# First cross-attention's attending loop: two tiles in a row, four buffers of probabilities and values, loops unrolled

## The reference

```python
def _L0_xattn_ref(x, latents, gamma_x, beta_x, gamma_l, beta_l, Wq, Wkv, Wo):
    xn = layer_norm(x, gamma_x, beta_x)          # x: the context, 12544 x 256
    ln = layer_norm(latents, gamma_l, beta_l)    # 128 x 256
    q = (ln @ Wq).reshape(b, m, h, d)            # h = 8 heads, d = 64
    kv_x = xn @ Wkv
    k_x = rope_rotate_k(k_x)                     # the context's keys
    ...
    k = jnp.concatenate([k_x, k_l], axis=2)      # context, then latents
    v = jnp.concatenate([v_x, v_l], axis=2)
    sim = jnp.einsum('bhid,bhjd->bhij', q, k)
    attn = jax.nn.softmax(sim, axis=-1)
    out = jnp.einsum('bhij,bhjd->bhid', attn, v)
    return out @ Wo
x = x + _L0_xattn_ref(ctx_1024, _layernorm(x, axis=-1), ...)
```

## Time and profile before

| | |
|---|---|
| median of 3 executions | 2609.48 us (2606.8 to 2609.7) |
| the profiled execution | 2611.38 us, span of the trace 2609.4 us |
| the loop of `attend` in the trace | from 377.84 us (first values) to 782.97 us (end of the last sum) |
| records of values, scores and weights matmuls of context tiles | 392, 1568, 1568 |
| mean granted clock of TensorE | 0.936 of 2.4 GHz over the span |

### The profile page before, as it was taken

One profiled execution on the slowest core, in us unless ns is written; L12 is line 12 of the kernel. 1 busy time (PEld: TensorE's weight loads), 2 busy tenths in 40 slices (PEclk: granted clock), 3 DMA queues, 4 the chain that ended last, 5 costly groups with the idle time before them and its releaser, 6 DMA issues. The chain is left out here.

```text
span 2609.4 us, 57414 instructions
## 1 busy us (share of the span) xinstructions
PE 2324.1 (89%) x21898; PEld 1435.1 (55%) x21898; DVE 1837.8 (70%) x2825; ACT 1194.8 (46%) x2046; POOL 518.1 (20%) x300
## 2 busy tenths in 40 slices
PE   3999989999994969999987999999997459999979
PEld 1444446666664836666656745665555415555548
DVE  6888778988886166666634388888886777777721
ACT  4566543333334337777772333333332325556552
POOL 0555530000000030000001065555562010000000
PEclk7999989999997969999997999999998769999989
DMA  8676855566544667667724422222211356676644
GB/s 271 213 250 234 273 178 155 167 170 194 167 133 165 210 156 165 152 163 163 166 59 155 151 99 99 98 98 98 98 57 47 97 130 146 155 161 147 147 137 168
DMA packets 245680, 397.63 MB, mean 152 GB/s; under 512 B 28905, under 2 KB 210288, under 8 KB 245396
## 3 DMA queue, kind: packets, MB, share of 16 engines
q1 hardware_dynamic: 239860, 393.90, 52.8%
q10 hardware_dynamic: 5664, 1.44, 0.3%
HBM read 316.44 MB, written 78.06 MB: 151 GB/s over the span
## 5 line engine op out<-in xcount | busy, mean ns | idle before, releaser
L1629 DVE CUSTOM_DVE_ANT_0 l3x_junk<-l3x_pm,l3x_mrow,l3x_top 128x896 bf16<-128x896 f32 x224 | 246.1, 1148 | 89.5 <-PE l3x_pm L1785 89.0
L1713 ACT ACTIVATE l1x_prob<-l1x_ring,mask_col 128x512 f32<-128x512 f32 x392 | 247.9, 684 | 120.0 <-PE l1x_ring L1805 118.9
L1716 ACT ACTIVATE l3x_prob<-l3x_ring 128x512 f32<-128x512 f32 x392 | 213.1, 595 | 162.7 <-PE l3x_ring L1809 162.7
L1163 ACT ACTIVATE l0x_att_pt<-l0x_att_pt 128x1024 f32<-128x1024 f32 x99 | 104.7, 1058 | 254.7 <-DVE l0x_att_pt L1098 254.7
L2778 POOL TENSOR_TENSOR l2x_gk<-l2x_f,first_vin 128x1024 f32<-128x1024 f32 x98 | 184.2, 1916 | 161.3 <-DVEq L2519 161.3
L1208 PE MATMUL l0x_att_pv<-l0x_wv,l0x_att_vin 128*128 128x512 f32 x392 | 195.0, 620 | 0.0
L2652 PE MATMUL l2x_kf<-l2w_w,l2x_nin 128*128 128x512 f32 x392 | 173.6, 603 | 4.5 <-DVE l2x_f L2493 4.5
L2652 PE MATMUL l2x_kf<-l2w_w,l2w_first 128*128 128x512 f32 x392 | 171.3, 597 | 0.0
L2493 DVE SCALAR_TENSOR_TENSOR l2x_f<-l2x_kf,l2x_rs,l2w_bias 128x1024 f32<-128x1024 f32 x98 | 125.8, 1284 | 57.7 <-PE l2x_kf L2652 45.4
L1629 DVE CUSTOM_DVE_ANT_0 l1x_junk<-l1x_pm,l1x_mrow,l1x_top 128x896 bf16<-128x896 f32 x112 | 123.7, 1148 | 57.3 <-PE l1x_pm L1785 57.3
L1629 DVE CUSTOM_DVE_ANT_0 l1x_junk<-l1x_pm,first_mrow,l1x_top 128x896 bf16<-128x896 f32 x112 | 123.4, 1148 | 54.6 <-PE l1x_pm L1785 54.6
(11 more groups left out here) (732 smaller groups left out, 4953.7 us busy)
## 6 DMA issues: line engine op xcount, KB each, us to landing
first_kt<-scratch_KS SPq DMA_DIRECT2D x84, 448.0 KB, 9.1
scratch_KT<-l0x_max_kf SPq DMA_DIRECT2D x28, 896.0 KB, 4.7
l0x_att_kt<-scratch_KT SPq DMA_DIRECT2D x56, 448.0 KB, 7.1
scratch_KS<-l0x_side_kp SPq DMA_DIRECT2D x14, 1344.0 KB, 13.5
l1x_kt<-scratch_KS SPq DMA_DIRECT2D x42, 448.0 KB, 9.4
scratch_KS<-first_kt SPq DMA_DIRECT2D x14, 1344.0 KB, 5.9
l3x_kt<-scratch_KS SPq DMA_DIRECT2D x42, 448.0 KB, 8.8
l0fw_w<-L_ffn_exp_w SPq DMA_DIRECT2D x16, 1024.0 KB, 7.6
```

The costliest lines, as they stand in the source:

```text
L1629: dve.tensor_tensor_reduce(junk[x % 2][:, :, :], pm[x % 2][:, :, 0:SPLIT], mrow[b][:, :].rearrange("p (s k) -> p s k", s=2), 1.0, top[1 - ...
L1713: ins = act.activation(into, scores, ACT.Exp, bias=R.mask_col[:, bass.ds(m * TILES + n // 4, 1)])
L1716: ins = act.activation(into, scores, ACT.Exp)
```

## The change

TensorE works on pairs of tiles: `begin(i, t)` issues the scores of t and t+1 and then the values of both, and the loop issues `begin` for the next pair, then the weights of t and t+1. VectorE takes per pair two subtractions, two value tiles, the two sums of the pair *before*, then the side halves. ScalarE takes two exponentials, then the side halves. `pt` and `v` have four buffers, tile mod 4; `psc` and `pv` keep two. The buffer of `top_wide` is now `pt[3]`. All loops of TensorE, VectorE and ScalarE are unrolled in the program text, and each of these engines waits once for `counts_started`, which GpSimd raises after `start_counts`. The last two sums come after the loop. The kernel's code for 16 heads and for masks in this function, which nothing else calls, is partly dropped.

```diff
-            v = [sb(f"v{b}", [P, heads, vd]) for b in range(2)]
+            v = [sb(f"v{b}", [P, heads, vd]) for b in range(4)]
...
-        pt = [sb(f"pt{b}", [P, 8, P]) for b in range(2)]
+        pt = [sb(f"pt{b}", [P, 8, P]) for b in range(4)]
...
-            top_wide = sb("top_wide", [P, heads, P])
+            top_wide = pt[3]
...
+        def buffer(i, t):
+
+            return (i * per_body + t) % 4
...
                 def subtract(i, t):
 
                     u, j = octet_counts(i, t, 0)
+                    at = buffer(i, t)
                     after(dve, sem(f"scores{u}"), j + 1)
-                    after(dve, *weighed(i, t, 0))
-                    after(dve, sem(f"summed{u}"), j)
-                    dve.tensor_tensor(pt[u][:, :, :], psc[u][:, :, :].rearrange("p a (b q) -> p (a b) q", q=P),
+                    if j >= 2:
+                        after(dve, sem(f"weighed{u}"), j - 1)
+                        after(dve, sem(f"summed{u}"), j - 1)
+                    dve.tensor_tensor(pt[at][:, :, :], psc[u][:, :, :].rearrange("p a (b q) -> p (a b) q", q=P),
                                       tops[:, :, :], ALU.subtract).then_inc(sem(f"shifted{u}"), 1)
...
+                dve.wait_ge(S.sem("counts_started"), 1)
+                for i in range(steps):
+                    dve.sem_inc(S.sem("values_begun"), 1)
+                    dve.tensor_copy(rs[:, :], R.rs[:, i * per_body:(i + 1) * per_body]).then_inc(sem("rs"), 1)
+                    after(dve, sem("rs"), i + 1)
+                    for t in range(0, per_body, 2):
+                        two = (t, t + 1)
+                        for n in two:
+                            subtract(i, n)
+                        for n in two:
+                            tile(i, n)
+                        for n in two:
+                            if n >= 2:
+                                weights_sum(i, n - 2)
+                            elif i:
+                                weights_sum(i - 1, per_body - 2 + n)
+                        for n in two:
+                            beside(i, n)
                     side.low_half(dve, i, 1, 1)
...
+                for n in (per_body - 2, per_body - 1):
+                    weights_sum(steps - 1, n)
+                subtract(steps, 0)
+                weights_sum(steps, 0)
...
+                for i in range(steps):
+                    for t in range(0, per_body, 2):
+                        exps(i, t)
+                        exps(i, t + 1)
...
+                def begin(i, t):
+
+                    for n in (t, t + 1):
+                        scores(i, n, 0)
+                    for n in (t, t + 1):
+                        values(i, n)
+
+                pe.wait_ge(S.sem("counts_started"), 1)
+                scores(0, 0, 0)
+                values(0, 0)
+                values(0, 1)
+                clear()
+                pe.wait_ge(S.sem("tops"), 1)
+                scores(0, 1, 0)
+                for i in range(steps):
+                    for t in range(0, per_body, 2):
+                        if t + 2 < per_body:
+                            begin(i, t + 2)
+                        elif i + 1 < steps:
+                            begin(i + 1, 0)
+                        for n in (t, t + 1):
+                            weigh(i, n, 0)
...
+                pool.sem_inc(S.sem("counts_started"), 1)
```

More of the change, by code:

```diff
@@ L1132, in _ @@
[L1132 to L1151 removed]
+                    if j >= 2:
+                        after(dve, sem(f"weighed{vb}"), j - 1)
@@ new lines, in tile, with beside @@
+                    after(dve, sem(f"v_proj{vb}"), j + 1)
+                    dve.scalar_tensor_tensor(v[buffer(i, t)][:, :, :],
+                                             pv[vb][:, 0:heads * vd].rearrange("p (h d) -> p h d", h=heads),
+                                             rs[:, t:t + 1], bias_v[:, :].rearrange("p (h d) -> p h d", h=heads),
+                                             ALU.mult, ALU.add).then_inc(sem(f"v{vb}"), 1)
+                def beside(i, t):
+                    s = t % TILES
+                    if s in (3, 5):
+                        side.rest_half(dve, i, t // TILES, (s - 3) // 2)
+                    if s == 5:
+                        side.low_half(dve, i, t // TILES, 0)
+                    if t == TILES:
+                        side.low_half(dve, i, 0, 1)
@@ L1178, in _ @@
-                act.activation(first_exp[:, :], R.ident[:, 0:1], ACT.Exp)
-                with act.Fori(0, steps) as i:
-                    for t in range(per_body):
-                        for o in range(octets):
-                            exps(i, t, o)
-                        s = t % TILES
-                        if s in (2, 4):
-                            side.high(act, i, t // TILES, s // 2 - 1)
-                        if s in (4, 6):
-                            side.middle_half(act, i, t // TILES, s // 2 - 2)
@@ L1188, in _, with exps @@
-                if last_tile:
-                    exps(steps, 0, 0)
+                def exps(i, t):
+                    u, j = octet_counts(i, t, 0)
+                    into = pt[buffer(i, t)]
+                    after(act, sem(f"shifted{u}"), j + 1)
+                    act.activation(into[:, :, :], into[:, :, :], ACT.Exp).then_inc(sem(f"probs{u}"), 1)
+                act.activation(first_exp[:, :], R.ident[:, 0:1], ACT.Exp)
+                act.wait_ge(S.sem("counts_started"), 1)
+                for i in range(steps):
[3 more added lines that the diff above has]
+                        for n in (t, t + 1):
+                            s = n % TILES
+                            if s in (2, 4):
+                                side.high(act, i, n // TILES, s // 2 - 1)
+                            if s in (4, 6):
+                                side.middle_half(act, i, n // TILES, s // 2 - 2)
@@ L1191, in _ @@
+                exps(steps, 0)
             @block.tensor
@@ L1248, in weigh @@
                         after(pe, sem(f"v{vb}"), jv + 1)
-                    vv = v[vb] if vals is None else vals
+                    vv = v[buffer(i, t)] if vals is None else vals
                     for k in range(8):
@@ L1257, in weigh @@
                             lhs = vv[:, h, :]
-                        last = pe.matmul(out, lhs, pt[u][:, h // 2 + 4 * (h % 2) if wide else k, :], start=False, stop=False, skip_group_check=True)
+                        last = pe.matmul(out, lhs, pt[buffer(i, t)][:, h // 2 + 4 * (h % 2), :], start=False, stop=False, skip_group_check=True)
                     done, n = weighed(i, t, o)
```

87 lines of the change are left out of this document (2 added, 85 removed).

## The result

The changed kernel takes **2577.51 us** (median of 4, 2575.03 to 2578.71) against 2608.22 for the kernel before (median of 4). The ratio is 0.9881, 95% interval 0.9864 to 0.9898: 31 us faster, where 26 were forecast.

The account below looks back on a forecast made before the run. TensorE's own sequence was taken as the bound, at 4.03 us per tile. 391.4 + 353.0 + 3.6 + 8.7 = 756.7 against 782.97 takes 26 us off 2611.4; less 1.9 for the median, 2583.5 us, range 2580 to 2594.

Parts of the forecast that it names:

- the attending stage: Stage of the changed loop, from VectorE's first `attend` instruction to the last sum's end: forecast 26 us less.
- The pair at 7.51 us: TensorE in the loop: two tiles pay three shape changes instead of six, 2 × 3.48 + 0.55 = 7.51 us.
- the free boundary inside a pair: TensorE between two groups of one shape, such as scores to scores: taken as costing 0, despite its semaphores.
- VectorE that just fits: VectorE in a body of seven pairs: 51.0 us of work against TensorE's 52.6, with 1.6 us of room.
- no wait of TensorE's matmuls: TensorE in the loop: no wait expected even with VectorE 3.5 us late at worst; the four buffers permit it.
- the tail of 8.7: End of the stage, from last scores' start to last sum's end, through VectorE: 8.7 us, where before took 5.3.
- the end of the last sum at 756.7: End of the stage: 391.4 + 353.0 + 3.6 + 8.7 = 756.7, against 782.97 before.
- Both rivals of TensorE and VectorE: TensorE: half-array boundaries still cost, 2601 us, chance 0.08. VectorE: becomes the bound, 2593 us, chance 0.08.
- the tail that the Trainium skill gives: TensorE boundaries inside pairs: about 60 ns at each of 147, 9 us of the gain, time 2592 us.
- Nothing runs beside this stage but its own transfers and what follows starts at its end, so all of it reaches the time.: Whole kernel: the stage's 26 us gain reaches the measured time in full.
- the starting point: Time of the kernel before: median of the runs 2609.5 us, 1.9 lower than the profiled execution's 2611.4.
- All three count nothing: Attending stage: unrolled loops, the wait for GpSimd's counts and the borrowed fourth buffer each neither cost nor earn time.

Follow-up runs that it names:

- run 5: Kernel before with 32 one-element memsets added on VectorE in an idle time of the first feed-forward stage: 2602.72 us, ratio 0.9981.
- run 10: Kernel before with 64 one-element memsets at an idle place of VectorE in the first feed-forward stage: 2602.42 us, ratio 0.9988.
- run 12: Kernel before with a single one-element memset at an idle place of VectorE in the first feed-forward stage: 2604.24 us, ratio 0.9989.
- run 8: Changed kernel with 100 one-element memsets at an idle place of VectorE in the first feed-forward stage: 2576.62 us, ratio 0.9877.
- run 9: Changed kernel with 68 one-element memsets at an idle place of VectorE in the first feed-forward stage: 2577.98 us, ratio 0.9884.
- run 13: Changed kernel with 63 one-element memsets at an idle place of VectorE in the first feed-forward stage: 2577.93 us, ratio 0.9883.
- run 1: Kernel before with only the attending function's loops unrolled and the one wait for the counts: 2602.55 us, ratio 0.9986.
- run 2: Changed kernel, but TensorE takes scores, values, scores, values of a pair, then the weights of both: 2595.72 us, ratio 0.9961.
- run 3: Changed kernel with the last tile's subtraction put ahead of the last side half and last two sums on VectorE: 2575.40 us, ratio 0.9886.
- run 11: Changed kernel with 66 idle-place memsets and one 128 x 2200 memset ahead of the first feed-forward stage's last copy: 2581.90 us, ratio 0.9909.
- run 6: Kernel before with 128 one-element memsets at an idle place of VectorE in the first feed-forward stage: 2606.90 us, ratio 0.9997.
- run 4: Kernel before, unchanged, measured once more for a second trace: 2609.04 us.

## Why the prediction was wrong

**Right, to a fraction of a microsecond: the attending stage.** The pair at 7.51 us, the free boundary inside a pair, VectorE that just fits (50.2 us busy in 52.6), no wait of TensorE's matmuls from 400 to 740 us, the tail of 8.7 (8.8), the end of the last sum at 756.7 (758.21, in an execution whose stage began 0.9 us later). The stage gave 25.6 us of 26. Both rivals of TensorE and VectorE are excluded by the rows above. By the tail that the Trainium skill gives in "TensorE: Matmul & The Clock Gate", section "The cost: per-tile semaphore tail", a pair would have needed about 0.2 us more (an estimate by its formula, three boundaries of 60 ns). The trace, at 7.51 us, does not agree for boundaries at which the next group has the same shape. By the Trainium skill's "TensorEngine Tiling (Array Packing)", section "Key Properties", a change of tiling mode drains TensorE. The trace agrees that the cost lies at the changes, 0.14 to 0.20 us each; that it is a drain, it does not show.

**Wrong: "Nothing runs beside this stage but its own transfers and what follows starts at its end, so all of it reaches the time."** The step takes the rest of the kernel as fixed. It isn't. 6.0 us separate forecast and result. A part of them is the starting point: I had started from the 2609.48 us of three executions; the kernel before took 2608.22 with one more, which is 1.3 us, and 2605.5 to 2607.2 beside the later runs. The stage gave 0.4 less than forecast. The remaining **5.1 us** (30.7 − 25.6) are the stages behind the loop, and by the later medians of the kernel before only 2.4 to 4.1. The interval of the ratio alone would allow 1 to 10.

Against the kernel before with its cuts moved (0.9981, 0.9988, 0.9989 in runs 5, 10 and 12, which leave the loop alone) the changed kernel and its variants 8, 9 and 13 (0.9881, 0.9877, 0.9884, 0.9883) gain 0.0105 on average, 27 us, the stage and little else. So the kernel before carried a loss of 2.5 to 5 us that has nothing to do with attending: a cut between two blocks of VectorE's instructions that fell right behind a wait. An edit ahead of it that adds 1, 32 or 64 VectorE instructions takes it away, one that adds 128 does not.

The working named the unrolling and gave it a price, "All three count nothing". It was read inside the stage only, and from TensorE alone. Inside the stage it holds, to 0.01 us (run 1). For the code behind it is worth some 4 us in the second cross-attention's stage (run 1: 447.61 to 443.45). And the traces have a second such piece, in the third cross-attention, which the memsets do not touch. Its stage, cut in the same way, before, in run 12 and in run 1:

```profile
1480.45:2000.36 519.91, 507.04 (x4044) 300.97 (x4044) 428.90 (x499) 161.10 (x176) 284.31 (x126) 0.98 0.25 88
...
1474.64:1994.32 519.68, 506.96 (x4044) 301.04 (x4044) 428.75 (x498) 161.10 (x176) 284.33 (x126) 0.98 0.25 88
...
1472.58:1991.14 518.56, 506.61 (x4044) 300.96 (x4044) 428.24 (x499) 161.16 (x176) 284.45 (x126) 0.98 0.25 88
```

It takes 519.6 to 519.9 us in all seven traces with the looped text, whatever the memsets, 518.5 to 518.7 in runs 1, 2, 3, 8, 9 and 11, and 517.2 and 517.3 in the changed kernel and run 13. So about 1.1 us go with the unrolled text, and not with where VectorE's cuts fall.

**Shown** is that the cut makes the instruction late and that the late instruction is needed for both stretches of low clock (runs 5, 6, 10, 12). **Open** is why the stretches fail to come in run 13; where the third cross-attention's 1.1 us come from (the unrolling moves the text of ScalarE and TensorE too, which no run varied by itself); why the changed kernel's own second cross-attention takes 444.85 and its variants 442.75 to 444.82; and what the other later stages give, of which the fourth layer's cross-attention alone differs by 2.6 us between two executions of one kernel (run 4).

## What to carry to other kernels

Order work on TensorE by shape: where buffers allow, put two groups of one shape in a row, and price each change of shape that disappears, not each group. And a stage that an edit doesn't touch is not a constant: where engines wait for each other at many places, the number of instructions ahead of it can decide which of them comes late. Before crediting a few tenths of a per cent to an edit, compare the untouched stages of both traces; if they differ, add one idle instruction to the kernel before and see what that is worth. And take the kernel before from more than three executions when the range of the forecast is a few us wide.

## What the runs showed of the hardware that I had not expected

- VectorE's cuts repeat every 128 instructions (128 more bring the late instruction back, 1, 32 and 64 don't), and the packet that moves with them has 8 KB. Crossing from one block into the next can be seen: 0.36 us where the cut lies right behind a wait (runs 12 and before), nothing where it lies ahead of it (run 12). The Trainium skill's "Runtime: NRT & Kernel Launch", section "Instruction fetch mechanics", speaks of blocks of 16 KiB, 256 instructions, whose crossing is mostly hidden. The trace agrees with "mostly", and for VectorE not with the size.
- 0.36 us late on VectorE cost 4.0 us in the kernel before: two stretches of 3.4 us at 1.2 GHz, the second 174 us behind the first, each worth about 1.7 us, half its length. In run 13 the same lateness brought neither stretch.
- A change of shape on TensorE costs 0.14 to 0.20 us in each of the four directions seen here (scores to values, values to scores, values to weights, weights to scores), and a boundary between equal half-array groups, with its semaphores, costs nothing that can be measured.
